# Turning the sampling matrix of a deformable convolution by DMA instead of by TensorE

## The chip, the cores and the metric

The kernel runs on one core of one Trainium2 chip. The metric is the device time of one execution in microseconds (us). TensorE (PE) multiplies matrices into PSUM, VectorE (DVE), ScalarE (ACT) and GpSimd (POOL) work elementwise, SyncE (SP) issues DMAs. Each engine works through its own instructions in order; semaphores tie them together.

## What is computed

32 images of 192 channels by 32 x 32 pixels go through channel attention and then a modulated deformable 3 x 3 convolution, each behind a group norm and with a residual; batch norm (over all 32 images) and GELU end it.

```python
x = x + attention(_gn(x))                 # q k^T over channels: 192 x 192 per image
x = x + deform(_gn(x))

def deform(x):                            # K = 9 taps
    offset = clip(_conv(x, off_w, off_b), -8, 8)
    mask = 2 * sigmoid(_conv(x, mask_w, mask_b))
    p = sum over 4 corners of  x[at the corner] * (bilinear weight * valid * mask)
    y = einsum('bckhw,ock->bohw', p, w) + b
    return gelu(batch_norm(y, over all images and pixels))
```

## The kernel before

Bilinear sampling is done as a matrix product. An image has 8 tiles of 128 pixels and 8 chunks of 128 source pixels. **Z** is a chunk of the normalized image times the projection weights, for a row of taps (`ky`) and its three `kx`: 128 source pixels by 576. **S** holds the sampling weights of a tile's 128 output pixels over 8 source rows by 32 columns, that is 256 source pixels in two halves of 128 (`c`), for three `kx`. S times Z, summed over taps and chunks, is the output (`acc`). Both are split in a high and a low float16 part, and three of the four products are formed.

Work of an image goes in 48 **units** `u` = (tile, `ky`, `c`). In each unit:

- PE `turn_s` (L666) turns three 128 x 128 float32 blocks of S of unit u+2 into PSUM bank `sps[u % 2]`, since POOL makes S with output pixels on the partitions (L1343, 128 x 768 for two units, tile `sT`) and the product wants source pixels there;
- ACT `split_s` (L905) casts them to `sh`, DVE `split_s` (L1161) subtracts to get `sl`;
- PE `convolve` (L683 to L685) does nine matmuls of 192 columns with `sh`, `sl`, `zh`, `zl`;
- PE `z_group` (L652 to L656) does five matmuls of 288 columns, a half of a Z piece, ten units ahead, into `zps[g % 2]`; ACT `split_z` (L871) casts it to `zh`, DVE `split_z` (L1155) makes `zl`. PE waits for `z_lo` of the group before last.

Behind the unit's own work stands `part0(u)`, a unit of the **preparation** of the next image: group norm, attention (gram matrix at u = 16 and 17, softmax at 18 to 20, its products at 21 and 22, applied at 23 to 26), second group norm (28), the images shifted by a pixel (`move`, DVE, u = 33, 35 and 36, L1024 to L1028, the last one raises `x2_moved`), the offset convolution on PE (u = 38 and 39, four tiles each, L594) and from u = 40 the hat functions `ay` and `bx` from which POOL makes S. An operation of u on one engine mostly waits for one of u or u-1 on another. `part1` writes out units and preparation for each engine; a loop runs over the images, two in a body. Image 0 is prepared alone, and image 31 runs without preparation. Then batch norm and GELU read y back from HBM and write the output.

SP stores and loads images (`attended`, `convolved`), nothing else.

```python
for u in range(UNITS):            # PE, part1
    turn_s(u + 2, b)
    convolve(u, b, par)
    z_group(u + AHEAD, b, par)    # AHEAD = 10 units
    if more:
        part0(u, b + 1, 1 - par)
```

Of the kernel before, what the change touches and what calls it, by code (L numbers as in the profile page):

```python
# [31 lines left out]
ALU = mybir.AluOpType  # L32
# [3 lines left out]
P = 128  # L36
# [15 lines left out]
UNITS = 6 * TILES  # L52
HEAD_SCALE = float((C // 4) ** (-0.5))
# [29 lines left out]
def build(nc, x, w_qkT, w_v, w_outT, b_out, w_off, b_off, w_proj, proj_b, gamma, beta,  # L83
# [6 lines left out]
    with ExitStack() as ctx:  # L90
# [76 lines left out]
        ST_RING = 3  # L167
        sT = sb("sT", [P, ST_RING, 3, R * W])
        S_RING = 3
        sh = sb("sh", [P, S_RING, 3, P], F16)  # L170
        sl = sb("sl", [P, S_RING, 3, P], F16)
# [13 lines left out]
        zps = bank("zps", (P, 2, 512))  # L185
        sps = [bank(f"sps{i}") for i in range(2)]
# [56 lines left out]
        s_ps = sem("s_ps")  # L243
        s_hi = sem("s_hi")
        s_lo = sem("s_lo")
        sz_done = sem("sz_done")
# [89 lines left out]
        def images(program, eng):  # L336
# [8 lines left out]
            part1(0, 0, True)  # L345
            with nc.Fori(1, NB - 2, 2, engines=bass.OrderedEngineSet([eng.engine]), hint_back_edge=True) as b:
                part1(b, 1, True)
                part1(b + 1, 0, True)
            part1(NB - 1, (NB - 1) % 2, False)
# [8 lines left out]
        AHEAD = 10  # L358
        FAR_Z = 2 * AHEAD
        FAR_SLOT = S_RING - 1  # L360
# [8 lines left out]
        def z_piece(z, g, par):  # L369

            half = g % 2 * (KO // 2)
            return z[:, tile_at(g // 6, par), g % 6 // 2, half:half + KO // 2]
# [52 lines left out]
        def _(sp):  # L425
            def load_x(b):
                for dst, src in ((xin[:, 0], x[b, 0:P]), (xin[0:CB, 1], x[b, P:C]), (xin[CB:P, 1], x[b, P:C])):
                    sp.dma_start(dst, src).then_inc(x_loaded, 16)
# [9 lines left out]
            def attended(b, more=True):  # L438
                sp.wait_ge(x1_sb, 4 * b + 4)
                sp.dma_start(x1_dram[b, 0:P], x1[:, 0]).then_inc(x1_stored, 16)  # L440
                sp.dma_start(x1_dram[b, P:C], x1[0:CB, 1]).then_inc(x1_stored, 16)
                if more:
                    load_x(b + 1)

            def convolved(b):
                sp.wait_ge(y_final, b + 1)
                sp.dma_start(y_dram[b, 0:P], ych[:, 0]).then_inc(y_stored, 16)
                sp.dma_start(y_dram[b, P:C], ych[0:CB, 1]).then_inc(y_stored, 16)

            attended(0)  # L450
            with sp.Fori(1, NB - 2, 2) as b:
                attended(b)
                convolved(b - 1)
# [956 lines left out]
```

## Time and profile before

| | us |
|---|---|
| median of 3 runs | 4003.83 (3988.3 to 4007.59) |
| the profiled execution, time | 3993.97 |
| its span, first to last instruction | 3992.2 |
| PE busy | 3544.1 (89%) |
| DVE busy | 2646.4 (66%) |
| ACT busy | 2111.3 (53%) |
| POOL busy | 1412.8 (35%) |

Busy time of PE is the union of instructions that overlap in its pipeline: a matmul of 192 columns is shown as 246 ns long, but the next starts some 80 ns later. For what a stretch of matmuls costs, starts have to be compared. Idle time before an instruction is put down to what released it.

### The profile page before, as it was taken

How to read it: one execution, taken by the hardware profiler on the slowest of the kernel's cores; microseconds unless marked ns; L12 is line 12 of the kernel's file. 1: busy time of each engine (PE TensorE's matmuls, PEld its weight loads, DVE VectorE, ACT ScalarE, POOL GpSimd, SP SyncE). 2: the span in 40 equal slices, each digit the busy share in tenths (PEclk: the TensorE clock that was granted, in tenths of full speed). 3: DMA queues.
4: the chain of work that ended last, by engine and by line, in shares of the span. 5: the costliest groups of instructions: out<-in, count | busy, mean ns of one | idle time of the engine just before them, and what ended most of it. 6: DMA issues, size and time to landing. Idle time of an engine off the chain costs nothing.

```text
span 3992.2 us, 110012 instructions
## 1 busy us (share of the span) xinstructions
PE 3544.1 (89%) x38338; PEld 3034.8 (76%) x38338; DVE 2646.4 (66%) x5834; ACT 2111.3 (53%) x4790; POOL 1412.8 (35%) x1165
## 2 busy tenths in 40 slices
PE   3999999999999999999999999999999999999700
PEld 2788887888888888888888888888888888888700
DVE  3577766676677667677766676677667667766522
ACT  1555555565555555555555565555555555555432
POOL 1333333343433333333333343333333333333311
PEclk8999999999999999999999999999999999999955
DMA  2000000000000010000000000000000001000299
GB/s 63 20 10 28 28 27 22 28 28 19 20 28 28 20 28 28 28 10 28 28 20 28 28 28 15 23 28 28 20 28 28 28 10 28 28 20 18 76 377 322
DMA packets 50722, 170.05 MB, mean 43 GB/s; under 512 B 9664, under 2 KB 10880, under 8 KB 50176
## 3 DMA queue, kind: packets, MB, share of 16 engines
q1 hardware_dynamic: 39584, 136.75, 11.2%
q0 software_dynamic: 7168, 25.17, 1.6%
q8 instruction: 337, 5.52, 0.6%
q14 instruction: 209, 1.71, 0.1%
q10 hardware_dynamic: 3424, 0.90, 0.1%
HBM read 87.29 MB, written 75.50 MB: 41 GB/s over the span
## 4 chain that ended last, share of the span: by engine, by line
PE 66%; DVE 12%; issue 9%; DMA 4%; POOL 3%; ACT 3%; DVEq 1%; SPq 1%; ACTq 0%; POOLq 0%
PE sps L666 10%; PE acc L683 6%; PE acc L685 6%; PE acc L684 6%; PE l L594 4%; PE zps L652 3%; PE zps L656 3%; PE zps L653 3%; PE zps L655 3%; PE zps L654 3%; DVE zl L1155 3%; DMA xn<-x_scratch 2%; POOL sT L1343 2%; DVE sl L1161 2%; PE l L526 2%
## 5 line engine op out<-in xcount | busy, mean ns | idle before, releaser
L1343 POOL TENSOR_TENSOR sT<-ay,bx 128x768 f32<-128x768 f32 x768 | 1149.5, 1507 | 1363.4 <-PE sps L666 1292.5
L1161 DVE TENSOR_TENSOR sl<-sps,sh 128x384 f16<-128x384 f32 x1536 | 846.0, 551 | 563.8 <-ACT sh L905 557.7
L683 PE MATMUL acc<-zh,sh 128*128 128x192 f16 x4608 | 1133.7, 246 | 0.9 <-issue 0.6
L685 PE MATMUL acc<-zh,sl 128*128 128x192 f16 x4608 | 1133.6, 246 | 0.0
L684 PE MATMUL acc<-zl,sh 128*128 128x192 f16 x4608 | 1133.6, 246 | 0.0
L905 ACT CAST sh<-sps 128x384 f16<-128x384 f32 x1536 | 741.7, 483 | 695.3 <-PE sps L666 689.6
L871 ACT CAST zh<-zps 128x288 f16<-128x288 f32 x1536 | 620.4, 404 | 638.8 <-PE zps L656 611.7
L1155 DVE TENSOR_TENSOR zl<-zps,zh 128x288 f16<-128x288 f32 x1536 | 693.2, 451 | 334.3 <-ACT zh L871 325.4
L666 PE MATMUL sps<-eye,sT 128*128 128x128 f32 x4608 | 785.8, 279 | 127.2 <-DVE sl L1161 99.4
L666 PEld LDWEIGHTS sps<-eye,sT 128*128 128x128 f32 x4608 | 530.9, 140 | 283.5 <-DVE sl L1161 167.9
L684 PEld LDWEIGHTS acc<-zl,sh 128*128 128x128 f16 x4608 | 450.9, 98 | 17.7 <-issue 0.8
L683 PEld LDWEIGHTS acc<-zh,sh 128*128 128x128 f16 x4608 | 450.8, 98 | 2.4 <-DVE sl L1161 0.5
L685 PEld LDWEIGHTS acc<-zh,sl 128*128 128x128 f16 x4608 | 450.9, 98 | 0.0
L652 PE MATMUL zps<-wpr_h,x_hi_a 128*128 128x288 f16 x1344 | 384.6, 286 | 1.0 <-DVE zl L1155 0.6
L653 PE MATMUL zps<-wpr_l,x_hi_a 128*128 128x288 f16 x1344 | 384.4, 286 | 0.0
L654 PE MATMUL zps<-wpr_h,x_lo_a 128*128 128x288 f16 x1344 | 384.4, 286 | 0.0
L655 PE MATMUL zps<-wpr_h,x_hilo_b 128*128 128x288 f16 x1344 | 384.4, 286 | 0.0
L656 PE MATMUL zps<-wpr_l,x_hilo_b 128*128 128x288 f16 x1344 | 384.4, 286 | 0.0
L1327 POOL TENSOR_TENSOR bx<-off,cx_sb 128x576 f32<-128x576 f32 x128 | 155.5, 1215 | 459.0 <-DVE off L1122 459.0
L1309 POOL TENSOR_TENSOR rstd<-gvar,mhalf 128x2 f32<-128x2 f32 x64 | 44.9, 702 | 553.9 <-DVE gvar L1012 553.9
L594 PE MATMUL l<-wof,x2s_hi_a 128*128 128x54 f16 x1536 | 182.8, 186 | 9.8 <-DVE x2w_hilo_b L1028 9.8
L594 PE MATMUL l<-wof,x2s_lo_a 128*128 128x54 f16 x1536 | 182.6, 186 | 0.0
(200 smaller groups left out, 6482.7 us busy)
## 6 DMA issues: line engine op xcount, KB each, us to landing
xin<-in_x SPq DMA_DIRECT2D x32, 512.0 KB, 5.4
xin<-in_x SPq DMA_DIRECT2D x64, 256.0 KB, 6.0
x_scratch<-x SPq DMA_DIRECT2D x32, 512.0 KB, 2.7
y_scratch<-ych SPq DMA_DIRECT2D x32, 512.0 KB, 2.7
zh<-y_scratch SPq DMA_DIRECT2D x20, 512.0 KB, 11.1
zl<-x_scratch SPq DMA_DIRECT2D x20, 512.0 KB, 12.5
out<-zh POOLq DMA_DIRECT2D x20, 512.0 KB, 8.6
x_scratch<-x SPq DMA_DIRECT2D x32, 256.0 KB, 3.4
```

Of the source, the lines that this page charges most:

```text
L594: mm = pe.matmul(o, src[:, row * W:(row + ROWS_T) * W], wof[:, m, k].rearrange("p i j -> p (i j)"), start=(k == 0 and n == 0), stop=(k == ...
L652: pe.matmul(o, at(0), wpr_h[:, 0, ky, n], start=True, stop=False)
L653: pe.matmul(o, at(0), wpr_l[:, 0, ky, n], start=False, stop=False)
L666: mm = pe.transpose(sps[u % 2][:, kx * P:(kx + 1) * P], sT[:, g, kx, c * P:(c + 1) * P], eye32[:, :])
L683: pe.matmul(acc[:, 0:C], s_h, zh[:, j, ky, z], start=start and kx == 0, stop=False)
L684: pe.matmul(acc[:, 0:C], s_h, zl[:, j, ky, z], start=False, stop=False)
L685: mm = pe.matmul(acc[:, 0:C], s_l, zh[:, j, ky, z], start=False, stop=stop and kx == 2)
L871: act.copy(z_piece(zh, g, par), zps[:, g % 2, 0:KO // 2]).then_inc(z_hi, 1)
L905: act.copy(sh[:, u % S_RING].rearrange("p k n -> p (k n)"), sps[u % 2][:, 0:3 * P]).then_inc(s_hi, 1)
L1155: dve.tensor_tensor(z_piece(zl, g, par), zps[:, g % 2, 0:KO // 2], z_piece(zh, g, par), ALU.subtract)\
L1161: dve.tensor_tensor(one(sl), sps[u % 2][:, 0:3 * P], one(sh), ALU.subtract).then_inc(s_lo, 1)
L1343: pool.tensor_tensor(sT[:, p % ST_RING].rearrange("p k (r x) -> p k r x", r=R), a, x_, ALU.mult)\
```

## The change

Turning S leaves PE. POOL writes S as float32 into `s32` (128 x 768, one **step** p = two units), ACT casts it and DVE subtracts while output pixels are still on the partitions (`spm`, 128 x 2 x 768 float16, ring of 2), and SP issues one DMA transpose per step that turns all twelve 128 x 128 blocks, high and low, SBUF to SBUF, into `sT` (ring of 4 slots). There are 24 steps per image, 768 in all. PE waits for the transpose's own semaphore. The two PSUM banks of `sps` go to `zps`, so Z is evicted 576 wide, 24 times per image on each engine. The work is written in steps; Z runs 5 steps ahead, splitting and turning 3 steps ahead, POOL 4. Preparation is shifted by 6 units (`SHIFT`): behind step p stand `part0(2p + 6)` and `part0(2p + 7)`, and units 0 to 5 of the image after the next behind steps 21 to 23. The offset convolution stands at u = 37, 38, 39 with 2, 3 and 3 tiles. SP's stores and loads now stand at step 5 (y) and at u = 36 (x), in one queue with the transposes.

```diff
+STEPS = 3 * TILES
+SHIFT = 6
-        AHEAD = 10
+        AHEAD = 5
+        S_AHEAD = 3
+            def turn_s(p, b):                                    # SP
+                sp.wait_ge(s_lo, STEPS * b + p + 1)
+                if p >= T_RING or not first(b):
+                    sp.wait_ge(sz_done, STEPS * b + p - T_RING + 1)
+                sp.dma_start_transpose(sT[:, p % T_RING], spm[:, p % S_RING].rearrange("p i n -> p (i n)"))\
+                  .then_inc(turned(b, p)[0], 16)
...
-                if 38 <= u < 40:
-                    for t in range(TILES // 2):
-                        offset_conv(TILES // 2 * (u - 38) + t, b, par)
+                if 37 <= u < 40:
+                    for t in ((0, 1), (2, 3, 4), (5, 6, 7))[u - 37]:
+                        offset_conv(t, b, par)
...
-            def turn_s(u, b):                                    # PE
-                for kx in range(3):
-                    mm = pe.transpose(sps[u % 2][:, kx * P:(kx + 1) * P], sT[:, g, kx, c * P:(c + 1) * P], eye32[:, :])
+            def convolve(p, b, par):
+                pe.wait_ge(*turned(b, p))
+                for c in range(2):
+                    mm = s_product(lambda lo, kx: sT[:, p % T_RING, 6 * lo + 2 * kx + c], ...)
...
+                for p in range(STEPS):                           # PE, part1
+                    convolve(p, b, par)
+                    z_group(p + AHEAD, b, par)
+                    for u in (2 * p, 2 * p + 1):
+                        prepare(part0, u, b, par, more)
...
+            def split_s(p, b):                                   # ACT
+                act.wait_ge(st_made, STEPS * b + p + 1)
+                if p >= S_RING or not first(b):
+                    act.wait_ge(*turned(b, p - S_RING))
+                act.copy(spm[:, p % S_RING, 0], s32[:, p % S_RING]).then_inc(s_hi, 1)
...
+            def split_s(p, b):                                   # DVE
+                dve.wait_ge(s_hi, STEPS * b + p + 1)
+                dve.tensor_tensor(spm[:, p % S_RING, 1], s32[:, p % S_RING], spm[:, p % S_RING, 0], ALU.subtract)\
+                   .then_inc(s_lo, 1)
...
+            def make_s(p, b, par):                               # POOL
+                if p >= S_RING or not first(b):
+                    pool.wait_ge(s_lo, STEPS * b + p - S_RING + 1)
```

Two places in the order of instructions. First VectorE around the last `move`, whose last copy (`x2w_hilo_b`) lets TensorE begin the offset convolution. Before, from unit 34 to unit 36 of the preparation:

```order
L1161 TENSOR_TENSOR sl<-sps,sh 128x384 [waits s_hi]
L1155 TENSOR_TENSOR zl<-zps,zh 128x288 [waits z_hi]
L1024 COPY x2s_lo_a<-x_lo_a 128x32x31 [waits xn_lo]
L1025 COPY x2s_lo_a<-x_lo_a 128x32x31
L1027 COPY x2w_lo_a<-x_lo_a 128x96
L1028 COPY x2w_lo_a<-x_lo_a 128x96
L1161 TENSOR_TENSOR sl<-sps,sh 128x384 [waits s_hi]
L1155 TENSOR_TENSOR zl<-zps,zh 128x288 [waits z_hi]
L1024 COPY x2s_hilo_b<-x_hilo_b 128x32x31
L1025 COPY x2s_hilo_b<-x_hilo_b 128x32x31
L1027 COPY x2w_hilo_b<-x_hilo_b 128x96
L1028 COPY x2w_hilo_b<-x_hilo_b 128x96
```

The same place in the changed kernel (step 15; L1193 is the low part of S, L1188 that of Z, L1255 the scaling of y):

```order
L1060 COPY x2w_lo_a<-x_lo_a 128x96
L1061 COPY x2w_lo_a<-x_lo_a 128x96
L1192 ISA
L1193 TENSOR_TENSOR spm<-s,spm 128x768 [waits s_hi]
L1187 ISA
L1188 TENSOR_TENSOR zl<-zps,zh 128x576 [waits z_hi]
L1250 ISA
L1255 TENSOR_SCALAR ych<-yt,unscale,pb 128x256 [waits yt_ps]
L1255 TENSOR_SCALAR ych<-yt,unscale,pb 128x256
L1057 COPY x2s_hilo_b<-x_hilo_b 128x32x31
L1058 COPY x2s_hilo_b<-x_hilo_b 128x32x31
L1060 COPY x2w_hilo_b<-x_hilo_b 128x96
```

The wider splits and a scaling of y now stand between the second and the third `move`.

Second TensorE ahead of the product with the softmax (u = 21), which waits for `prob_sb` of VectorE's u = 20. Before, the rows from the unit's Z group on:

```order
L652 MATMUL zps<-wpr_h,x_hi_a 128x288 [waits z_lo]
L653 MATMUL zps<-wpr_l,x_hi_a 128x288
L654 MATMUL zps<-wpr_h,x_lo_a 128x288
L655 MATMUL zps<-wpr_h,x_hilo_b 128x288
L656 MATMUL zps<-wpr_l,x_hilo_b 128x288
L619 REGISTER_ALU
L525 MATMUL l_1<-wo,gram 128x192 [waits prob_sb]
```

Now, from the end of step 7's Z group on:

```order
L704 MATMUL zps<-wpr_l,x2w_hilo_b 128x288
L730 ISA
L732 REGISTER_ALU [waits y_pm]
L734 REGISTER_ALU [waits flag_sb]
L737 MATMUL yt<-eye,ypm 128x128 [waits y_ch]
L738 MATMUL yt<-eye,ypm 128x128
L737 MATMUL yt<-eye,ypm 128x128
L738 MATMUL yt<-eye,ypm 128x128
L666 REGISTER_ALU
L572 MATMUL l_1<-wo,gram 128x192 [waits prob_sb]
```

Before, a whole unit of PE work lay between PE's place for u = 20 and that for u = 21; now both stand behind the same Z group, with only the turning of y ahead of them.

## Rows read from the trace of the kernel before

**Rows 1.** The page, its parts 1 and 2: busy time, and granted clock in 40 slices.

```profile
PE 3544.1 (89%) x38338; PEld 3034.8 (76%) x38338; DVE 2646.4 (66%) x5834; ACT 2111.3 (53%) x4790; POOL 1412.8 (35%) x1165
...
PEclk8999999999999999999999999999999999999955
```

**Rows 2.** Timeline of SP (start us, us, ...): a store of x1, 23 images apart.

```profile
878.85 0.34 SPq L440 DMA_DIRECT2D x_scratch<-x  x1
...
3530.61 0.35 SPq L440 DMA_DIRECT2D x_scratch<-x  x1
```

**Rows 3.** Groups by line and shape: xcount | busy us, mean ns | idle before <-releasers.

```profile
L1343 POOL TENSOR_TENSOR sT<-ay,bx 128x768 f32<-128x768 f32 x768 | 1149.5, 1507 | 1363.4 <-PE sps L666 1292.5 <-DVE ay L1137 37.1 <-ACT bx L864 33.7
...
L1161 DVE TENSOR_TENSOR sl<-sps,sh 128x384 f16<-128x384 f32 x1536 | 846.0, 551 | 563.8 <-ACT sh L905 557.7 <-issue 3.1
L666 PE MATMUL sps<-eye,sT 128*128 128x128 f32 x4608 | 785.8, 279 | 127.2 <-DVE sl L1161 99.4 <-POOL sT L1343 17.3 <-issue 2.7
L905 ACT CAST sh<-sps 128x384 f16<-128x384 f32 x1536 | 741.7, 483 | 695.3 <-PE sps L666 689.6
L1155 DVE TENSOR_TENSOR zl<-zps,zh 128x288 f16<-128x288 f32 x1536 | 693.2, 451 | 334.3 <-ACT zh L871 325.4
L871 ACT CAST zh<-zps 128x288 f16<-128x288 f32 x1536 | 620.4, 404 | 638.8 <-PE zps L656 611.7
```

**Rows 4.** Timeline of one unit on PE: turn, product, Z, next turn.

```profile
1001.72 0.49 PE L666 MATMUL sps<-eye,sT 128*128 128x128 f32 x3
...
1002.05 0.25 PE L683 MATMUL acc<-zh,sh 128*128 128x192 f16 x1
...
1002.79 0.29 PE L652 MATMUL zps<-wpr_h,x_hi_a 128*128 128x288 f16 x1
...
1003.40 0.49 PE L666 MATMUL sps<-eye,sT 128*128 128x128 f32 x3
```

**Rows 5.** Busy time by engine in two images: start:end, length, PE, PEld, DVE, ACT, POOL, clock.

```profile
994.50:1225.70 231.20, 221.30 (x2404) 189.72 (x2402) 161.53 (x362) 128.01 (x296) 85.36 (x68) 1.00 0.09 25
```

**Rows 6.** Operations with all inputs in SBUF, by line: ns min/median/max; ACT's as in rows 3.

```profile
L1018 DVE TENSOR_TENSOR xl_a<-xn,xh_a x32: 1224/1710/1716, 46.7 to 3596.3; 128x1024 f16<-128x1024 f32 x32
...
L1018 DVE TENSOR_TENSOR x_hilo_b<-xn,x_hilo_b x32: 1222/1222/1224, 94.2 to 3663.0; 64x1024 f16<-64x1024 f32 x32
...
L804 ACT ACTIVATE xn<-x,nbias,rstd 128x1024 f32<-128x1024 f32 x64 | 80.5, 1258 | 13.8 <-POOL nbias L1313 13.8
```

**Rows 7.** Timeline: one small DVE copy beside a POOL product, and one without.

```profile
1009.37 1.69 POOL L1343 TENSOR_TENSOR sT<-ay,bx 128x768 f32<-128x768 f32 x1 [2.23 <-PE sps L666]
...
1009.66 1.45 DVE L1027 COPY x2w_hi_a<-x_hi_a 128x96 f16<-128x96 f16 x1
...
1017.13 0.41 DVE L1024 COPY x2s_hilo_b<-x_hilo_b 128x992 f16<-128x992 f16 x1
...
1017.82 0.17 DVE L1027 COPY x2w_hilo_b<-x_hilo_b 128x96 f16<-128x96 f16 x1
```

**Rows 8.** DMA issues: xcount, KB each, median us from issue to landing.

```profile
xin<-in_x SPq DMA_DIRECT2D x32, 512.0 KB, 5.4
...
x_scratch<-x SPq DMA_DIRECT2D x32, 512.0 KB, 2.7
```

**Rows 9.** The attention chain: a group by shape, then three places of the timeline.

```profile
L525 PE MATMUL l<-wo,gram 128*128 128x192 f32 x64 | 19.2, 382 | 21.5 <-DVE gram L1075 21.5
...
1077.69 0.36 DVE L1056 COPY gram<-l 128x192 f32<-128x192 f32 x1 [1.27 <-PE l L555]
...
1089.99 1.05 DVE L1075 TENSOR_SCALAR gram<-gram,rinv 128x192 f32<-128x192 f32 x2
...
1097.58 0.56 DVE L1080 TENSOR_TENSOR mt_l<-l,mt_h 128x384 f16<-128x384 f32 x1 [1.68 <-ACT mt_h L840]
```

**Rows 10.** Timeline: u = 32 on DVE, a scaling of y, the first offset matmul.

```profile
1004.70 0.99 DVE L1223 TENSOR_SCALAR ych<-yt,unscale,pb 128x256 f32<-128x256 f32 x2
...
1006.51 1.71 DVE L1018 TENSOR_TENSOR x_lo_a<-xn,x_hi_a 128x1024 f16<-128x1024 f32 x1
...
1019.28 0.19 PE L594 MATMUL l<-wof,x2s_hi_a 128*128 128x54 f16 x1
```

More of the change, by code:

```diff
@@ L184, in build @@
         yt = bank("yt")
-        zps = bank("zps", (P, 2, 512))
-        sps = [bank(f"sps{i}") for i in range(2)]
+        zps = bank("zps", (P, 4, 512))
         l0 = [bank(f"l0_{i}") for i in range(2)]
@@ L242, in build @@
         st_made = sem("st_made")
-        s_ps = sem("s_ps")
         s_hi = sem("s_hi")
         s_lo = sem("s_lo")
+        lo_seen = sem("lo_seen")
+        slot_free = sem("slot_free")
+        s_turned = [sem(f"s_turned{i}") for i in range(T_RING)]
         sz_done = sem("sz_done")
@@ L344, in images, with prepare @@
                     weights_ready()
[L345 to L349, printed above, removed]
+            for u in range(SHIFT):
+                part0(u, 1, 1)
+            part1(0, 0, 2)
+            with nc.Fori(1, NB - 4, 2, engines=bass.OrderedEngineSet([eng.engine]), hint_back_edge=True) as b:
+                part1(b, 1, 2)
+                part1(b + 1, 0, 2)
+            for b in range(NB - 3, NB):
+                part1(b, b % 2, min(2, NB - 1 - b))
+        def prepare(part0, u, b, par, more):
+            if u + SHIFT < SLOTS:
+                if more:
+                    part0(u + SHIFT, b + 1, 1 - par)
+            elif more == 2:
+                part0(u + SHIFT - SLOTS, b + 2, par)
         far_bodies = []
@@ L678, in s_product @@
-            def s_product(slot, j, ky, start, stop):
+                for h in range(2):
+                    o = z_bank(g)[:, h]
+                    n = slice(h * KO // 2, (h + 1) * KO // 2)
+                    pe.matmul(o, at(0), wpr_h[:, 0, ky, n], start=True, stop=False)
+                    pe.matmul(o, at(0), wpr_l[:, 0, ky, n], start=False, stop=False)
+                    pe.matmul(o, at(1), wpr_h[:, 0, ky, n], start=False, stop=False)
+                    pe.matmul(o, at(2), wpr_h[:, 1, ky, n], start=False, stop=False)
+                    mm = pe.matmul(o, at(2), wpr_l[:, 1, ky, n], start=False, stop=True)
@@ L700, in far_pass @@
             def far_pass(b, par, more):
-                pe.wait_ge(s_lo, UNITS * (b + 1) + 2 * more)
                 pe.wait_ge(y_ch, 4 * (b + 1))
```

300 lines of the change are left out of this document (145 added, 155 removed).

## The prediction

> **What bounds the kernel now.** The page first: PE is busy 89% of the span, DVE 66%, and the granted clock stands at its top (tenths 9, full speed; 1.00 in the two images of [rows 5]) from the second slice to the final phase [rows 1]. The stores of x1 give the length of an image: (3530.61 - 878.85) / 23 = 115.3 us [rows 2]; 31 images run at that pace, each with the preparation of the next beside it. In one pair of them PE is busy 221.3 of 231.2 us [rows 5]. So PE's order of instructions is the path, and I read off what a unit costs there: the turn takes 2.05 - 1.72 = 0.33 us, the nine products 0.74, the five Z matmuls 0.61, together 1.68 [rows 4]. 48 units are 81 us; some 30 are preparation, and 4 to 5 PE waits. Of its waits the largest are those before the turn: 127.2 us in all, 4.0 per image, mostly for DVE's low part of S [rows 3].
>
> **Part 1: the turn leaves PE.** 48 x 0.33 = 15.8 us per image. The waits before it go too, 4.0 per image, since nothing on PE waits for a PSUM bank of `sps` any more. Together 19.8 us per image, all on the path. A step (two units) of products and Z is now 2 x (0.74 + 0.61) = 2.70 us on PE.
>
> **Part 2: splitting S 768 wide from SBUF.** ACT: 1024 elements with inputs in SBUF took 1.258 us [rows 6], so 768 take about 0.95; before, two casts of 0.483 [rows 3]. DVE: 1024 elements with both inputs in SBUF took 1.222 us undisturbed [rows 6], so 768 take 0.92, before 2 x 0.551. A gain of small size on engines that aren't the bound. But the same subtraction took 1.71 where POOL was at work [rows 6], and a DVE copy of 96 elements took 1.45 us beside a POOL product and 0.17 without one [rows 7]: it ended when the product ended. The two engines shut each other out for some forms. Before, the low part of S read one input from PSUM and took 0.551 in the mean although POOL was at work 35% of the time [rows 1, 3]; now it has two SBUF inputs, so it falls under this. I charge it half a POOL product, 0.75 (between 0 and 1.5, POOL's 1.507 of [rows 3]).
>
> The Trainium skill says the same in "Advanced Engine Details and Errata", section GPSIMD Details: POOL shares an interface with DVE and conflicts with DVE instructions in a 2-port mode or with two SBUF inputs. It speaks against this part; by [rows 6, 7] the trace agrees.
>
> **Part 3: Z evicted 576 wide.** From 288 to 384 elements ACT's cast grows by 0.079 us and DVE's subtraction by 0.100 [rows 3]; by these slopes 576 take ACT 0.64 and DVE 0.75, where two of 288 took 0.81 and 0.90. DVE's whole load: 161.53 / 2 = 80.8 us per image, less 48 x (0.551 + 0.451), plus 24 x (0.92 + 0.75 + 0.75) = 91 us. It has room under 111 us, not much. The ring of Z is two groups as before, now of double size: PE may be two steps ahead of DVE.
>
> **Part 4: the DMA transpose.** No row shows one. It carries 128 x 1536 float16, 384 KB. Plain DMAs of 512 KB took 2.7 us (store) and 5.4 (load) from issue to landing [rows 8]; by bytes 2.0 is the lower bound, 5.4 the upper one of these rows, and nothing excludes more for a turned pattern. I take 4.0, nearer to the load. It counts through a loop: `spm` has two slots, so the cast for step p + 2 waits for the transpose of p. Loop: cast 0.95 + low part 0.92 + POOL 0.75 + transpose 4.0 + some 0.5 behind other work on ACT = 7.1 us for two steps, 3.6 per step. The image needs 111 / 24 = 4.6 per step, but unevenly: the twelve steps from 17 to the next image's 4 hold little preparation, some 37 us. PE can be fed three steps from the ring there, so 9 periods must fit: up to 4.1 per period, a transpose of 5.1 us. So at 4.0 it costs nothing; above 5.1 it costs 4.5 us per image for each us of latency. SP's stores and loads stand before transposes of steps 8 and 18 or 19, where PE waits or has three steps in store: nothing.
>
> The Trainium skill ("DMA: Bandwidth & Descriptors", section Latency and other measured facts) has 261 GB/s for a DMA transpose with a broken pattern. By it the 384 KB would move in 1.5 us, the loop would be shorter than mine, and the sum would not change. No run here shows it.
>
> **Part 5: the shift and the pairing of units.** This is what I charge most. Where before an operation of u on PE waited for u-1 on another engine, a unit of 1.68 us lay between. Now u = 2p and 2p + 1 stand together behind a step's products and Z, and on ACT and DVE they stand behind the split of that same Z, which ends 0.64 + 0.75 = 1.4 us after PE's Z. Per image PE will wait:
> - u = 17 for DVE's copy of the gram matrix, 0.36 and a short second one [rows 9]: 0.6.
> - u = 21: DVE's u = 20 starts 1.4 + 0.2 behind the Z of step 7, and takes 0.2 + 1.05 [rows 9]; PE has four turns of y in between, 0.4 at a third of 0.33 each [rows 4]: 2.5. Before, 21.5 us in 32 images, 0.7 each [rows 9].
> - u = 23 for `mt_lo`, right behind its source at u = 22: ACT's two casts of 384 and 128 columns (0.48 and, by the slope of part 3, 0.27) and DVE's 0.56 and a shorter one [rows 3, 9]: 1.5; before, a unit covered it.
> - u = 37 for `x2_moved`. Count from the start of step 13 on PE. ACT has 2 x 1.26 of normalizing and 1.6 of splits in each of steps 12 and 13, 4.1 against PE's 2.7; it starts the ones of step 12 when PE starts step 13 (they follow the cast of Z), so its cast of S of step 13 ends at 0.7 + 2.5 + 0.95 = 4.1, DVE's low parts of S and Z 1.7 later, at 5.8. Then DVE: residue, behind POOL, to 7.9; move 0.9 (the undisturbed one runs from 1017.13 to 1018.0, [rows 7]), 8.8; step 14's splits behind ACT's, 10.4; residue 1.22 behind POOL, 12.4; move, 13.3; step 15's splits, 15.0; scaling of y, 0.99 [rows 10], 16.0; last move 0.9, with POOL ahead of it up to 17.3. PE is there after three steps, at 8.1, so it waits 8 (without POOL ahead of the last move) to 9.2. I take 9.2. Before, DVE ran from 1006.51 to about 1018 over the same operations, and the offset matmuls began at 1019.28 [rows 10], with hardly a wait of their own, because they stood two units behind the move; the 3 us lost there are among the 4.0 of part 1.
> - u = 12 behind a residue of 1.7 [rows 6], 1.2; and two more of this kind (u = 28 behind the moments, the turn of step 22 behind POOL's wait for the offsets), together 1.7, an estimate by the size of these.
>
> Sum 16.7; less the 1.0 that these places wait today, 15.7 net. The bounds: 0 if DVE and ACT run ahead by more than I think, and 20 if each wait behind POOL is a whole product.
>
> **The sum.** 19.8 - 15.7 = 4.1 us gained per image, 31 x 4.1 = 127 us. Against it, in the prologue six units of preparation stand uncovered and the first S goes through split and transpose before PE starts, about 8 us. Image 31 runs without preparation; its 24 steps at the loop's 3.6 less three in store take what 48 units take today, 81 us: nothing. The final phase is the same. 3994.0 (span 3992.2 and 1.8 around it) - 127 + 8 = 3875 for an execution like the profiled one; the median of the runs lies 10 us above it: **3885**.
>
> **Rivals.**
> - *The waits of part 5 are half of mine* (chance 0.20). For it: DVE is idle a third of the time today [rows 1], and delays that are added one by one, as here, may in part lie beside each other. Against: every row of the chain is measured. Then 4.1 + 8.3 = 12.4 per image: 3994 - 384 + 8 + 10, about 3630.
> - *The transpose is slow and becomes the bound* (0.18), the case on the other side. Price: with 7 us from issue to landing the period is 5.1, nine periods 46 us against 37 and PE short of S by 9 per image in place of nothing: 4.1 - 9 = -4.9, +152 us: about 4160. It decides from 6.0 us of latency on, where the 4.1 are eaten up. For it: twelve blocks per DMA are small pieces, and no row bounds them from above. Against: both plain DMAs of more bytes are under 6.
> - *DVE becomes the bound through POOL* (0.08). Each S split waits out a whole product: 91 + 24 x 0.75 = 109 us of DVE per image, and with the 8 us or so that it must wait for PE's gram and softmax products 117: +1.7 x 31 + 8 + 10, about 4065.
> - *The clock falls* (0.03). PE stands still 9 us in each image; the clock is at the lower level in the last slices, where PE has little to do [rows 1]. If each such stop cost a few us at 1.2 GHz, the gain would be gone: about 4060.
> - *It does nothing that counts* (0.04): the parts cancel, 3990 to 4020.
>
> **How the numbers follow.** My sum has the rest, 0.47, with its own range of 3780 to 4000. A measurement here can tell about 0.5% from no change, so faster means below 3984. Faster: 0.43 of the sum's 0.47, and 0.20 of the first rival, 0.63. Same: 0.03, the last rival's 0.04, and 0.05 of the cases in which the others are mild: 0.12. Slower: the rest, 0.25. The range of 3610 to 4120 leaves out the far half of the slow transpose and of the first rival.
>
> **What would show it.** Right: stores of x1 about 111 us apart; no L666 on PE; PE idle some 9 us before the first offset matmul, released by DVE's last move, and 2 to 3 before the softmax product; transposes landing in about 4 us, with no wait of PE for them in steps 0 to 16; DVE's low part of S well above 0.92 us in the mean. Wrong: transposes above 6 us, PE waiting for DMA in most steps, images above 115 us; or images at 103 us with the offset matmuls hardly waiting, which would mean that DVE's backlog in steps 13 to 15 is not what I worked out.

## The result and the profile after

The changed kernel takes **4368.97 us** in the median of 4 runs (4355.33 to 4388.95), beside 4002.81 (3988.3 to 4007.59) for the kernel before: ratio 1.0925, 95% interval 1.0874 to 1.0977. It is 9% slower. I had forecast 3885 and a range up to 4120, so both the sign and the range were wrong.

The page of the changed kernel, parts 1 and 2. Against [rows 1], PE's busy share fell from 89% to 76%, and the granted clock, steady at its top before, has eights among its nines all along.

```profile
PE 3327.8 (76%) x33730; PEld 2757.8 (63%) x33730; DVE 2413.0 (55%) x4298; ACT 1894.0 (43%) x3254; POOL 1442.3 (33%) x1165
...
PEclk8898899899898999999988999999998999888855
```

SP's stores of x1 (as [rows 2]), 21 images apart: (3261.51 - 602.51) / 21 = 126.6 us per image, before 115.3.

```profile
602.51 0.66 SPq L457 DMA_DIRECT2D x_scratch<-x  x1
...
3261.51 0.58 SPq L457 DMA_DIRECT2D x_scratch<-x  x1
```

Two images of it, columns as in [rows 5]:

```profile
1995.10:2247.90 252.80, 205.60 (x2108) 170.72 (x2108) 146.10 (x266) 114.24 (x200) 87.27 (x68) 0.91 0.54 97
```

Read this against [rows 5] per image. Before: 110.7 us busy and 5.0 idle. After: 102.8 busy and 23.6 idle, 126.4 in all. Without the turn's 15.8 us, PE should be busy 94.9 at full clock; the other 7.9 us are the lower clock (0.91 in the mean, 1.00 before). (The 94.9 rest on the 15.8 us that I read off one unit in [rows 4].) So the 10.8 us that an image got longer are made of -15.8 (the turn), +18.6 (idle) and +7.9 (clock). By the stores it is 11.3 per image, 350 of the 395 us between the two spans; the first product starts 12 us later (133.2 and 121.4), and the final phase, from the start of the last product on, is 31 us longer.

Where PE waits, from the waits of the changed kernel: who waited, for whom, us in total, times, longest.

```profile
PE acc L724 <- ACT ypm L961: 335.0, 98, 6.2
PE l L641 <- DVE x2w_hilo_b L1061: 112.0, 32, 9.8
PE l L572 <- DVE gram L1108: 95.7, 32, 3.4
PE l L564 <- DVE mv L1035: 83.3, 64, 14.2
PE l L627 <- DVE mt_l L1114: 48.9, 32, 1.5
...
PE acc L724 <- DMA sT<-spm: 7.6, 3, 6.5
```

The first row is the largest by far, and my prediction has no such term: before, the product (then L683) waited 0.3 us for this copy in the whole execution. It comes three times per image, 3.4 us each in the mean. L724 is the first matmul of a product. There is one accumulator `acc` in PSUM, and a tile's sum must be copied out of it (ACT, L960 and L961, into `ypm`) before the first product of the next tile. Here is one such place, first ACT, then PE (start us, us, engine, line, operation, [idle before]):

```profile
1979.53 1.24 ACT L838 ACTIVATE xn<-x,nbias,rstd 128x1024 f32<-128x1024 f32 x1
1980.67 1.23 ACT L829 ACTIVATE x_hi_a<-x,nbias,rstd 128x1024 f16<-128x1024 f32 x1
1981.80 0.82 ACT L938 CAST spm<-s 128x768 f16<-128x768 f32 x1
...
1984.39 1.24 ACT L838 ACTIVATE xn<-x,nbias,rstd 128x1024 f32<-128x1024 f32 x1
1985.53 1.23 ACT L829 ACTIVATE x_hilo_b<-x,nbias,rstd 128x1024 f16<-128x1024 f32 x1
1986.66 0.82 ACT L938 CAST spm<-s 128x768 f16<-128x768 f32 x1
1987.38 0.31 ACT L960 COPY ypm<-acc 128x192 f32<-128x192 f32 x1
1987.59 0.21 ACT L961 COPY ypm<-acc 128x64 f32<-128x64 f32 x1
```

```profile
1987.86 0.26 PE L724 MATMUL acc<-zh,sT 128*128 128x192 f16 x1 [3.05 <-ACT ypm L961]
...
1995.70 0.23 PE L641 MATMUL l<-wof,x2s_hi_a 128*128 128x54 f16 x1 [3.29 <-DVE x2w_hilo_b L1061]
```

ACT carries out two normalizations in each of two steps, 1.24 us apiece, and works without a pause; the copy of the tile, 0.5 us, stands behind all of it, and PE stands still. Before, the same four normalizations were spread over four units, each with PE's turn in it, and the copy was in time. Two of the three waits of an image are of this kind: 62 in the whole execution, 202 of the 335 us.

The third is another: 31 waits of 4.1 to 4.3 us, 128 us together. There ACT has no burst. It stands idle itself, for DVE's part of a row's hats (`ay`, L1159), which stands in DVE's queue behind the splits and the statistics of y, and the cast and the copy queue up behind it:

```profile
2019.25 0.44 ACT L887 ACTIVATE ay<-ay 128x288 f32<-128x288 f32 x1 [3.34 <-DVE ay L1159]
...
2020.11 0.81 ACT L938 CAST spm<-s 128x768 f16<-128x768 f32 x1
2020.83 0.31 ACT L960 COPY ypm<-acc 128x192 f32<-128x192 f32 x1
...
2021.31 0.26 PE L724 MATMUL acc<-zh,sT 128*128 128x192 f16 x1 [4.11 <-ACT ypm L961]
```

The splits and the transposes, by line (columns as in [rows 3]; the last row, of the issues, as in [rows 8]):

```profile
L1374 POOL TENSOR_TENSOR s<-ay,bx 128x768 f32<-128x768 f32 x768 | 1141.6, 1488 | 1969.5 <-DVE spm L1193 1613.2
...
L1193 DVE TENSOR_TENSOR spm<-s,spm 128x768 f16<-128x768 f32 x768 | 752.1, 979 | 627.0 <-ACT spm L938 620.5
L1188 DVE TENSOR_TENSOR zl<-zps,zh 128x576 f16<-128x576 f32 x768 | 579.4, 754 | 892.9 <-ACT zh L905 889.7
L905 ACT CAST zh<-zps 128x576 f16<-128x576 f32 x768 | 489.0, 637 | 1287.4 <-PE zps L704 1286.7
...
L938 ACT CAST spm<-s 128x768 f16<-128x768 f32 x768 | 639.5, 833 | 110.5 <-DMA sT<-spm 107.8
...
sT<-spm SPq DMA_TRANSPOSE x768, 3.7
```

And the clock, in stretches of 1 us behind that last wait (PE idle to 2021.31; the third figure from the end is the granted clock):

```profile
2021.00:2022.00 1.00, 0.69 (x9) 0.70 (x10) 1.00 (x2) 1.00 (x4) 0.01 (x1) 1.00 0.00 0
2022.00:2023.00 1.00, 1.00 (x11) 0.97 (x9) 1.00 (x2) 0.52 (x1) 1.00 (x1) 0.65 0.00 0
2023.00:2024.00 1.00, 1.00 (x7) 0.72 (x6) 0.93 (x6) 0.00 (x0) 0.47 (x1) 0.50 0.70 134
...
2026.00:2027.00 1.00, 1.00 (x15) 1.00 (x13) 0.44 (x1) 1.00 (x2) 0.20 (x1) 1.00 1.00 187
```

```profile
2022.62 0.37 PE L726 MATMUL acc<-zh,sT 128*128 128x192 f16 x1
2022.78 0.37 PE L724 MATMUL acc<-zh,sT 128*128 128x192 f16 x1
```

PE has begun again, works for about 1 us at full clock, and only then runs at 0.50, the level of 1.2 GHz, for about 3 us: matmuls of 192 columns start 0.16 us apart there (the two rows on PE), at full clock some 80 ns. In 74 of the 155 stops over 2.5 us of this trace the clock has already fallen when PE begins again, as at 2149.76. So a stop can be paid twice, once as idle time and once as slow work behind it, which the waits don't show.

### The profile page after: what moved, and what is told of

Same layout as the page of the kernel before. It is cut to its first block, busy times and chain, and to the rows that moved or that the text cites. A ratio compares the mean times of both kernels' runs of the same rounds, so it can differ in the third digit from the quotient of the medians.

```text
span 4387.3 us, 93414 instructions
## 1 busy us (share of the span) xinstructions
PE 3327.8 (76%) x33730; PEld 2757.8 (63%) x33730; DVE 2413.0 (55%) x4298; ACT 1894.0 (43%) x3254; POOL 1442.3 (33%) x1165
## 2 busy tenths in 40 slices
DMA packets 1254798, 470.63 MB, mean 107 GB/s; under 512 B 1213888, under 2 KB 1215104, under 8 KB 1254400
## 4 chain that ended last, share of the span: by engine, by line
PE 44%; DVE 15%; issue 14%; ACT 13%; DVEq 5%; DMA 5%; ACTq 3%; SPq 1%; POOL 0%; POOLq 0%
PE acc L724 6%; PE acc L725 5%; PE acc L726 5%; PE l L641 5%; ACT zh L905 3%; ACT spm L938 3%; PE zps L700 2%; DVE stats L1026 2%; PE zps L701 2%; PE zps L702 2%; PE zps L704 2%; PE zps L703 2%; DMA xn<-x_scratch 2%; ACT xn L838 2%; ACTq L897 2%
## 5 line engine op out<-in xcount | busy, mean ns | idle before, releaser
L1374 POOL TENSOR_TENSOR s<-ay,bx 128x768 f32<-128x768 f32 x768 | 1141.6, 1488 | 1969.5 <-DVE spm L1193 1613.2
L724 PE MATMUL acc<-zh,sT 128*128 128x192 f16 x4608 | 1232.9, 268 | 386.9 <-ACT ypm L961 335.0
L725 PE MATMUL acc<-zl,sT 128*128 128x192 f16 x4608 | 1233.8, 268 | 0.3 <-issue 0.3
L726 PE MATMUL acc<-zh,sT 128*128 128x192 f16 x4608 | 1233.3, 268 | 0.0
L1193 DVE TENSOR_TENSOR spm<-s,spm 128x768 f16<-128x768 f32 x768 | 752.1, 979 | 627.0 <-ACT spm L938 620.5
L1188 DVE TENSOR_TENSOR zl<-zps,zh 128x576 f16<-128x576 f32 x768 | 579.4, 754 | 892.9 <-ACT zh L905 889.7
L905 ACT CAST zh<-zps 128x576 f16<-128x576 f32 x768 | 489.0, 637 | 1287.4 <-PE zps L704 1286.7
L724 PEld LDWEIGHTS acc<-zh,sT 128*128 128x128 f16 x4608 | 489.6, 106 | 485.4 <-ACT ypm L961 319.6
L938 ACT CAST spm<-s 128x768 f16<-128x768 f32 x768 | 639.5, 833 | 110.5 <-DMA sT<-spm 107.8
L725 PEld LDWEIGHTS acc<-zl,sT 128*128 128x128 f16 x4608 | 490.9, 107 | 26.9 <-issue 0.5
L726 PEld LDWEIGHTS acc<-zh,sT 128*128 128x128 f16 x4608 | 494.6, 107 | 7.9
L641 PE MATMUL l<-wof,x2s_hi_a 128*128 128x54 f16 x1536 | 207.0, 195 | 112.0 <-DVE x2w_hilo_b L1061 112.0
L641 PE MATMUL l<-wof,x2s_hilo_b 128*128 128x54 f16 x1536 | 206.7, 195 | 0.8 <-issue 0.8
L960 ACT COPY ypm<-acc 128x192 f32<-128x192 f32 x256 | 81.4, 318 | 236.8 <-PE acc L726 236.1
## 6 DMA issues: line engine op xcount, KB each, us to landing
zl<-x_scratch SPq DMA_DIRECT2D x20, 512.0 KB, 11.3
```

Of the source, the lines that this page charges most:

```text
L641: mm = pe.matmul(o, src[:, row * W:(row + ROWS_T) * W], wof[:, m, k].rearrange("p i j -> p (i j)"), start=(k == 0 and n == 0), stop=(k == ...
L724: pe.matmul(acc[:, 0:C], s_h, zh[:, j, ky, z], start=start and kx == 0, stop=False)
L725: pe.matmul(acc[:, 0:C], s_h, zl[:, j, ky, z], start=False, stop=False)
L726: mm = pe.matmul(acc[:, 0:C], s_l, zh[:, j, ky, z], start=False, stop=stop and kx == 2)
L905: act.copy(z_piece(zh, g, par), z_bank(g)).then_inc(z_hi, 1)
L938: act.copy(spm[:, p % S_RING, 0], s32[:, p % S_RING]).then_inc(s_hi, 1)
```

## The experiments

My theory from these rows: the tile starts and the clock are what I missed; the transpose itself is innocent. The rivals: the transposes disturb the other engines or bound a loop; DVE, slowed by POOL, is behind it all; the waits for the preparation would keep PE as long if the tile starts went.

**Was the turn worth its length on PE?** The kernel before, with one turn of S per unit in place of three. Two thirds of S stay unturned, so its output is wrong. The edit:

```diff
-                for kx in range(3):
-                    mm = pe.transpose(sps[u % 2][:, kx * P:(kx + 1) * P], sT[:, g, kx, c * P:(c + 1) * P], eye32[:, :])
+                mm = pe.transpose(sps[u % 2][:, 0:P], sT[:, g, 0, c * P:(c + 1) * P], eye32[:, :])
```

> The kernel before with one 128 x 128 turn of S per unit on TensorE instead of three, which leaves out two thirds of the turning; order, splits and everything else stay. It asks what the removal alone is worth in the old order. My sum put a turn of three at 0.33 us on the path: two thirds in 48 units are 10.6 us per image, 31 images 330 us, so about 3675 if TensorE's work is the path. Theory 'TensorE's work hides the bursts of the others' (with less of it, the waits for ScalarE and VectorE come out): only half of that, 3800 to 3900. If the clock falls with TensorE's share of work, it is seen below 0.96 here as well.

Measured: 3807.4 us, ratio 0.9503 (0.9475 to 0.953). Two thirds of 15.8 us in 31 images would be 327 us; some 200 arrived. PE's busy time fell by 280 us (3544.1 to 3263.8) and its idle time grew by 92 (448.1 to 539.8). The idle time before the turn grew from the 127.2 of [rows 3]:

```profile
L665 PE MATMUL sps<-eye,sT 128*128 128x128 f32 x1536 | 453.6, 295 | 180.8 <-DVE sl L1162 155.3 <-POOL sT L1344 14.0 <-issue 6.5
```

So two things are missing from the 327: two turns cost PE's busy time less than two thirds of 0.33 us, and PE's work was also cover: with less of it per unit the other engines come late. That was the second theory of the expectation, and its range. With everything left in its place, though, the clock stays at 1.00 and most of the gain arrives.

**Are the transposes harmful in themselves?** The kernel before with 24 transposes per image of the changed kernel's shape, whose results nobody uses (it is also built with `dynamic_dma_scratch_size=4096`, as the changed kernel is):

```diff
+                    sp.dma_start_transpose(spare[:, p % 2], flat2(wpr_h).rearrange("p i n -> p (i n)")[:, 0:12 * P])\
+                      .then_inc(spared[p % 2], 16)
```

> The kernel before, with the DMA transposes added aside: in each image SyncE also issues 24 transposes of 128 x 1536 float16 from a constant tile into a spare one that nothing reads, one after each pair of low parts of S, two in flight at most. Nothing else is changed. Theory 'transposes disturb' (their traffic slows the engines, or itself lowers the granted clock): slower than before by 2% or more, clock below 0.95. Theory 'stops lower the clock, transposes are harmless': within 1% of before, clock 0.96 to 0.97; the transposes land in about 3.7 us as in the changed kernel.

Measured: 4015.58 us, ratio 1.0039 (1.0019 to 1.0059). They landed in 3.9 us in the median, 3.7 in the changed kernel. PE was busy 3545.9 us, before 3544.1, and its last product starts 3 us later (3774.1 and 3771.1). Transposes beside it cost PE next to nothing; most of the difference lies in the final phase, on which more at the end. And the loop through the transpose, with three slots of `spm` in place of two:

```diff
+        M_RING = 3
-        spm = sb("spm", [P, S_RING, 2, 3 * R * W], F16)
+        spm = sb("spm", [P, M_RING, 2, 3 * R * W], F16)
```

> The changed kernel with three slots of spm (the split S before it is turned) in place of two, so a cast of S waits for the transpose of three steps before. Theory 'the loop through the transpose is the bound': the period falls from (2 + 3.7 + queueing)/2 to a third, 3% or more faster, 4240 or less. Theory 'order of the work': the 107.8 us that ScalarE waits for the transpose go, TensorE's time barely moves: 4330 to 4380.

Measured: 4353.63 us, 1.0866 of before, where the changed kernel has 1.0925; the intervals overlap, and PE's wait for `ypm` is 329.9 us (335.0). ACT's wait for transposes fell from 107.8 us to 1.5, and PE's time barely moved: the loop doesn't bound the kernel.

**Is DVE, slowed by POOL, behind it?** The changed kernel with DVE's low part of S cut to 96 of 768 columns:

```diff
-                dve.tensor_tensor(spm[:, p % S_RING, 1], s32[:, p % S_RING], spm[:, p % S_RING, 0], ALU.subtract)\
+                dve.tensor_tensor(spm[:, p % S_RING, 1, 0:96], s32[:, p % S_RING, 0:96], spm[:, p % S_RING, 0, 0:96], ALU.subtract)\
```

> The changed kernel with VectorE's low part of S cut to 96 of its 768 columns (the rest of the low part is left out, zero): some 0.8 us less of VectorE's work per step with two inputs in SBUF, 19 us of VectorE per image. Theory 'VectorE and GpSimd in each other's way bound it': 5% faster or more, 4150. Theory 'order of the work': VectorE's work in the bursts gets shorter too, so some of the waits for it shrink, but those for ScalarE stay: 1 to 3% faster, 4240 to 4330.

Measured: 4310.91 us, 1.0784 of before. DVE's busy time fell by 559 us (2413.0 to 1854.4), the kernel by 58. DVE's load has a small part in it, as the theory 'order of the work' had it.

**The tile starts.** In the changed kernel each step's two units of preparation stand together. Pulled apart, on PE, ACT and DVE, one goes ahead of the Z group (and of its split) and one stays behind:

```diff
+                    prepare(part0, 2 * p, b, par, more)
                     if p + AHEAD < STEPS:
                         split_z(p + AHEAD, b, par)
...
-                    for u in (2 * p, 2 * p + 1):
-                        prepare(part0, u, b, par, more)
+                    prepare(part0, 2 * p + 1, b, par, more)
```

> The changed kernel with the two units of preparation of a step pulled apart: the first stands between the product (or the split of S) and Z on TensorE, ScalarE and VectorE, the second behind Z. Theory 'order of the work': what waits for the unit before gets TensorE's Z group, 1.2 us, as cover: the waits at u = 21, 23 and 37 shrink by some 1 us each per image, 3 us per image, 4270. Theory 'transposes' or 'port': no change, 4340 to 4400. A third outcome: ScalarE's and VectorE's splits of Z now stand behind a unit of preparation, so TensorE waits for Z instead, slower than 4370.

Measured: 4048.39 us, 1.0104 (1.0075 to 1.0134): 320 us of the 366 lost came back by order alone. My expectation had 4270, so it was right in its sign and far too small. The waits:

```profile
PE acc L724 <- ACT ypm L961: 178.1, 98, 4.9
PE l L564 <- DVE mv L1035: 158.7, 64, 14.2
PE l L641 <- DVE x2w_hilo_b L1061: 135.4, 32, 9.8
PE l L572 <- DVE gram L1108: 29.0, 32, 2.8
```

The tile starts, which the expectation didn't name, improve the most; the 31 of them that hang on DVE's hats fell from 128 us to 34. The softmax product (`gram`) improves too. The group statistics (`mv`) and the wait at u = 37 (112.0 before the edit), which I had expected to shrink, get worse. PE's busy time falls by 120 us, which I put down to the clock: the work is the same. The shift alone, 7 in place of 6:

```diff
-SHIFT = 6
+SHIFT = 7
```

> The changed kernel with SHIFT 7 in place of 6 and nothing else: the units that stand together become (2p+7, 2p+8), so the pairs (16,17), (20,21), (22,23), (36,37) are taken apart and (17,18), (21,22), (27,28), (3,4) are put together. Theory 'what stands together waits': TensorE's waits at u = 21, 23 and 37 (3.0, 1.5 and 3.5 us per image) shrink to below 1 us each, those before the group statistics (u = 4 and 28, L564, 2.6 us per image in the changed kernel) grow to 5 or more: net 3 us per image, about 4270. If only the number of units ahead counts, less than 1% changes.

Measured: 4194.26 us, 1.0493. The wait for `ypm` is 136.3, less than with units apart, but `mv` takes 181.7 and `xhl_b`, at u = 12, 87.1. The total came out better than the 4270 expected, again by the tile starts, which the expectation didn't name; the wait at u = 37 fell to 81.5 only. This run also says something of the clock: in its images from 700 to 3900 us no wait of PE is longer than 2.9 us, and still PE's busy time (3305.2 us) is little below the changed kernel's. Last, units apart and the tile's copy put ahead of ACT's cast of S:

```diff
+                    if p % 3 == 2:
+                        t = p // 3
+                        act.wait_ge(sz_done, STEPS * b + p + 1)
...
                     if p + S_AHEAD < STEPS:
                         split_s(p + S_AHEAD, b)
```

> The kernel with units pulled apart (4048), and ScalarE's copy of a finished tile out of the accumulator moved ahead of the cast of S in its step. TensorE there still waits 5.6 us per image at the start of a tile for this copy. Theory 'ScalarE comes late to the copy because of its bursts': the cast of S (0.83 us) no longer stands before it, 0.8 us less in some 3 waits per image, 2 us per image and a bit of clock: 3970 to 4000, faster than before. Against: the cast of S comes 0.5 us later, which costs nothing while S is three steps ahead. If the loop through the transpose is near its limit, it is 4040 to 4080.

Measured: 4154.17 us, 1.0392, so 2.6% slower than a_apart, a miss. The wait for `ypm` fell as the edit says, and others rose by more:

```profile
PE l L641 <- DVE x2w_hilo_b L1061: 172.9, 32, 9.8
PE acc L724 <- ACT ypm L953: 102.2, 92, 4.4
PE acc L724 <- DVE zl L1188: 65.3, 31, 2.5
```

By the order of instructions, ACT now waits for PE's product of this step before it casts S, which DVE and POOL wait for in turn; I take this for the cause, and no run takes it apart. The miss also says that less waiting for `ypm` isn't by itself a faster kernel: 76 us of it went here, and the kernel got slower.

**What does a stop cost by itself?** The kernel before, whose clock was at its top, with ten small DVE multiplications at u = 30 of every image:

```diff
+                if u == 30:
+                    for i in range(10):
+                        dve.drain()
+                        dve.tensor_tensor(spare[:, :], spare[:, :], spare[:, :], ALU.mult)
```

> The kernel before with a stop put in: once per image, at u = 30 of the preparation, VectorE does ten more small multiplications on a spare tile (some 6 us), so the low part of S comes late and TensorE stands still for several us. Nothing else is changed. Theory 'a stop of some us costs its length and then lowers the clock for a few us more': per image the length of TensorE's new wait plus 1.5 to 2 us, clock of the whole run below 0.95 (it is 0.966 without), and in the trace a granted clock of 0.5 behind each stop. With a new wait of 4 to 5 us per image: 4170 to 4220. Theory 'the lower clock comes with the changed kernel's other traits' (less work per unit of time on TensorE, transposes): only the wait's length, 4120 to 4160, clock 0.96.

Measured: 4241.44 us, 1.06 (1.056 to 1.0639), a little above the range of the first theory, since the stop came out at 6.5 us and not at 4 to 5. The stop in one image, the microsecond in which it ends, and the clock over 2000 us of steady work, first of this kernel, then of the kernel before:

```profile
1190.86 0.90 PE L667 MATMUL sps<-eye,sT 128*128 128x128 f32 x3 [6.53 <-DVE sl L1168]
```

```profile
1190.00:1191.00 1.00, 0.14 (x1) 0.14 (x2) 1.00 (x3) 0.00 (x0) 0.00 (x0) 0.50 0.00 0
```

```profile
1000.00:3000.00 2000.00, 1836.62 (x19504) 1575.47 (x19501) 1423.78 (x3087) 1051.40 (x2416) 696.65 (x553) 0.97 0.08 23
```

```profile
1000.00:3000.00 2000.00, 1913.28 (x20888) 1641.44 (x20887) 1397.23 (x3126) 1110.87 (x2569) 743.06 (x592) 1.00 0.08 24
```

PE's idle time grew by 162 us and its busy time, for the same matmuls, by 74 (3618.0 to 3544.1): 5.2 and 2.4 us per image. One stop per image in a kernel at full clock brings the clock down, with no other cause at hand. Here it falls in the stop, some 5 us after its start, and PE works at 0.50 for 5.6 us from 1190.86 on.

**One wait of the preparation taken back.** The changed kernel with the offset convolution in two parts again:

```diff
-                if 37 <= u < 40:
-                    for t in ((0, 1), (2, 3, 4), (5, 6, 7))[u - 37]:
-                        offset_conv(t, b, par)
+                if 38 <= u < 40:
+                    for t in range(TILES // 2):
+                        offset_conv(TILES // 2 * (u - 38) + t, b, par)
```

> The changed kernel with the offset convolution alone put back in two parts on two steps. Theory (the third part is what TensorE waits for at the offset matmuls, 3.5 us per image, and the stop costs about as much again in the clock): 4210 to 4290 us, with the wait of the offset matmuls below 40 us in all. Rival (the work before the offset maximum only crowds into one step less, and the wait moves to the hats or the tile starts): 4330 to 4390 us.

Measured: 4244.94 us, 1.0611 (1.0558 to 1.0664), with the wait for `x2_moved` at 30.9 us (before this edit 112.0) and that for `ypm` unmoved:

```profile
PE acc L724 <- ACT ypm L961: 337.3, 98, 6.1
```

PE's idle time fell by 74 us, and its busy time by another 67, although the work is the same. What b_stop showed holds in reverse: the stop gave its length back nearly twice. This was the first theory, and its range.

**A version that beats both.** Units apart, the group statistics on PE a unit later (u = 5 and 29), the offset convolution in two parts:

```diff
-                if u == 4:
+                if u == 5:
...
-                if u == 28:
+                if u == 29:
```

> The kernel with units pulled apart (4048 us), and two more waits given cover: TensorE's group statistics one unit later (u = 5 and 29 in place of 4 and 28, so that Z of the step lies before them), and the offset convolution in two parts of four tiles at u = 38 and 39 as before the change, in place of three parts from u = 37. These are the places where TensorE still stops for 5.0 and 4.2 us per image, long enough for the clock to fall behind them. Theory 'order of the work': each shrinks by 1.2 to 2.7 us, 3 to 4 us per image, and another 1 to 2 from the clock: 3860 to 3930, faster than the kernel before; clock above 0.93. If the waits only move on to the next place (the hats behind the later end of the offset convolution, the second normalization): 4000 to 4050.

Measured: **3870.71 us**, 0.9672 (0.9653 to 0.9692) of the kernel before and 11% below the changed kernel, in the range of the first theory (the clock of the four runs was 0.927 to 0.93, a little less than it had).

```profile
PE acc L724 <- ACT ypm L961: 207.3, 98, 5.2
PE l L564 <- DVE mv L1035: 82.8, 33, 14.2
PE l L641 <- DVE x2w_hilo_b L1061: 51.2, 29, 9.8
```

Three slots of `spm` on top of it:

> The same with three slots of spm in place of two, so that the cast of S waits for the transpose of three steps before. In the changed kernel this moved nothing (0.5%). With the order mended a step is shorter and ScalarE waits more for transposes (190 us with units pulled apart, against 108). Theory 'the loop through the transpose comes next': 1 to 2% faster than with two slots. Theory 'it stays hidden behind TensorE': within 0.5% of it.

Measured: 3854.63 us, 0.9633 (0.9602 to 0.9665); the intervals overlap, so this isn't told from a_v2. And a shift of 8 on top of a_v2:

> The version a_v2 (units of a step pulled apart, group statistics on their own steps, offset convolution in two parts) with a preparation shift of 8 instead of 6 and nothing else. Theory (what is left of the wait at the tile starts, 207 us for ScalarE's copy of the accumulator, is ScalarE coming late from its bursts): the shift moves the bursts against the tile starts, the wait falls by about half, some 3 us per image, and a little of the clock comes back: 3740 to 3800 us. Rival (the bursts only meet another tile start, or a wait for the group statistics or the offset matmuls grows instead): within 1% of a_v2, 3830 to 3910 us.

Measured: 3968.43 us, 0.9922 (0.9892 to 0.9952), a miss: 2.5% slower than a_v2. The first half of the theory held, the wait for `ypm` halved. But the waits inside the preparation grew by more, the one at u = 37 from 51.2 to 116.5 and the softmax product from 28.9 to 78.1. With 8 as with 6 the same units share a step; what changed is the main work that stands between them:

```profile
PE l L641 <- DVE x2w_hilo_b L1061: 116.5, 32, 9.8
PE acc L724 <- ACT ypm L961: 104.0, 85, 2.7
PE l L572 <- DVE gram L1108: 78.1, 32, 2.8
```

This was the rival's wording, though worse than its 1%. I haven't found which piece of the main work makes the difference.

Over all of them, PE's idle and busy time tell the story (us of one execution; the last column is busy time above the 3038.5 that 3544.1 - 32 x 15.8 leaves at full clock):

| | idle | busy | clock's part |
|---|---|---|---|
| changed kernel | 1059.5 | 3327.8 | 289 |
| narrow low part | 981.4 | 3326.3 | 288 |
| two parts | 985.4 | 3260.4 | 222 |
| shift 7 | 892.9 | 3305.2 | 267 |
| units apart | 839.1 | 3208.3 | 170 |
| v3 | 790.9 | 3172.8 | 134 |
| v2 | 723.5 | 3140.0 | 102 |

The last column's level rests on the 15.8 us of a turn, read off one unit; its differences don't. It doesn't follow the idle time everywhere: the narrow low part has 78 us less idle time than the changed kernel and as large a clock's part.

## Why the prediction was wrong

- **Part 1, the turn leaves PE: right about PE's work as far as the runs tell, wrong as a net gain.** 15.8 us of work went by the starts of [rows 4]; the run with one turn suggests somewhat less. The step counted it all as gained and put what it uncovered into part 5 alone.
- **Part 5, the list of waits, is the first of two steps that failed.** It went through the pairs of the preparation and left out a pair of the main work: ACT's copy of the tile and PE's next product, 10.5 us per image (335.0 / 32). All that was needed stood in my own item on u = 37. There I worked out that ACT has 4.1 us in each of steps 12 and 13 against PE's 2.7, and followed DVE behind it, but step 14 ends a tile, and its copy stands behind the same burst. The third of these waits, behind DVE's hats (128 of the 335 us), needed the same look at u = 40 and after, which the list doesn't reach. Of that item, DVE's time was right: the last `move` ends 17.3 us after the start of step 13 by my sum, 16.8 in the trace (1978.79 to 1995.55). PE's time was wrong: I had it there after 8.1, it came after 13.6, since it had stood 3.05 at the tile start and its third step took 4.6 us in place of 2.7, at a mean clock of 0.62 (1987.86 to 1992.41). So 3.3 us were left to wait where I had 9.2.
- **The other waits of part 5.** u = 21: 2.5 predicted, 3.0 measured. u = 23: 1.5 and 1.5. u = 17: 0.6 and 0.6. u = 12: 1.2, and next to nothing (4.2 us in ten images together). Two more of this kind, 1.7: the group statistics took 2.2 ((83.3 - 14.2) / 31) and the turn of the offset maximum 0.7. In sum 16.7 predicted, and 23.6 measured with the tile starts: 7 us too few.
- **The clock, a term put at nothing, is the second step that failed.** It was my rival of 0.03, sized at 4060 on its own. It is 7.9 us per image. I had seen that PE would stand still 9 us in an image, and that the clock stands lower where PE has little to do, and gave it no term because in [rows 5] it was 1.00. Nothing there stops long enough to show it: the waits for DVE's low part of S were 1.2 us at most. The Trainium skill ("TensorE: Matmul & The Clock Gate", Part 1: The HAM clock gate) has it that "the default state is throttled, and activity releases the throttle". The trace agrees: 0.50 behind the stop at 2021.31, 1.00 again after some 3 us of matmuls at 0.50. I should have weighed this rule in the prediction and didn't.
- Together: 111.2 us per image predicted, 126.6 measured; 7.9 of the difference is the clock and about 7 the waits. In 31 images that is 477 of the 514 us by which the profiled execution (4388.95) lies above my 3875; the final phase, which I had at no change, is 31. Added to 3885, the missed waits alone would give about 4100 and the clock alone about 4130. It took both to come to 4369, and they aren't independent: the stops are what brought the clock down.
- **Part 2, the charge for POOL: wrong.** The low part of S took 958 ns in the median and 979 in the mean, so some 0.05 and not 0.75 above the undisturbed 0.92. POOL's own row suggests why the rule didn't bite: POOL waits 1613.2 us for this very subtraction, since `s32` has two slots, so its product starts when the subtraction has ended and is mostly over when the next begins. The two do hinder each other when they meet: 100 of the 768 subtractions overlap a POOL instruction by more than 0.1 us; they took 1.15 us in the mean, the others 0.95. The longest one took 1697 ns. The Trainium skill's rule on the shared interface ("Advanced Engine Details and Errata", GPSIMD Details) stands by that, but a conflict needs both engines at work at the same time, which is a matter of this kernel's waits.
- **Part 3: right.** ACT 0.64 and DVE 0.75 predicted, 0.637 and 0.754 measured.
- **Part 4: right.** 4.0 us predicted, 3.7 measured; PE waits 7.6 us for transposes in the whole execution. The slow rival, a transpose above 6 us, didn't come: the sign came out as in it, the mechanism was another. That the kernel is slower was in my 0.25 for "slower", but by other mechanisms than those I had given it for.

What stays open: which length of stop brings the clock down. Most stops of this kernel at the tile starts and at u = 37, some 3 us and more, do, though not each: behind the one of 3.21 us that ends at 2051.26 it stayed at 1.00. Shorter ones do too: with a shift of 7 no wait of a steady image is above 2.9 us and the clock's part is still 267 us. With stops up to 1.4 us (the kernel with one turn) it stays at 1.00. The runs don't say where between, nor how much stops close to each other count together. Open too is what the tile starts are worth alone: no run takes away that wait and nothing else, as a second accumulator would.

## What to carry to other kernels

Work that leaves the busiest engine was also cover. Go through every pair in which that engine waits for another, those of the main loop's own buffers first (here one accumulator and its copy), and ask what stands ahead of the partner in its queue at that place. Charge a stop of TensorE of 2 or 3 us and more for more than its length (here 1.4 times in the mean, up to nearly twice), and spread bursts of the helpers over the steps before moving work: by order alone the same change went from 9% slower to 3% faster.

## What the runs showed of the hardware

- The clock can fall after a stop or in it. Behind the stop of 4.11 us PE worked at the full level for about 1 us, then about 3 us at 0.50. In the stop of 6.53 us it had fallen before PE began again, and 5.6 us of work at 0.50 followed. One such stop per image made PE's busy time 2.4 us longer.
- A DMA transpose of 128 x 1536 float16 from SBUF to SBUF landed in 3.6 us at least, 3.7 in the median and 8.9 at most; SP needed 1.43 us to issue one. 768 of them made 1,204,000 more packets (1,254,798 to 50,722) and PE's busy time in the kernel before didn't change by them. By the Trainium skill's 261 GB/s ("DMA: Bandwidth & Descriptors", Latency and other measured facts) the 384 KB would take 1.5 us, an estimate from the page's figure. The trace has more: from issue to landing they make 106 GB/s. By the packets' own times one transpose takes 2.4 us of all sixteen engines (56.7% of 4011.6 us with the unused ones, 11.2% of 3992.2 without, over 768), which is 165 GB/s, my estimate.
- The final phase, which has no transposes and the same operations, was longer in every kernel that had transposes before it: 237.5 to 252 us from the last product's start, against 219, 221 and 231 without. Here are the final phases of the kernel before, of it with the unused transposes, and of the changed kernel; DMA is fully busy in all three, and the last column is its rate in GB/s.

```profile
3780.00:3980.00 200.00, 0.00 (x0) 0.00 (x0) 54.68 (x49) 62.17 (x53) 33.35 (x61) 0.50 1.01 359
```

```profile
3795.00:4000.00 205.00, 0.00 (x0) 0.00 (x0) 52.31 (x46) 57.56 (x50) 32.94 (x60) 0.50 1.01 338
```

```profile
4150.00:4375.00 225.00, 0.00 (x0) 0.00 (x0) 52.43 (x45) 58.52 (x50) 32.85 (x60) 0.50 1.00 313
```

The same loads and stores go slower there. These are single executions, and what links them to the transposes isn't known; it wasn't tried further. Every kernel with transposes here was also built with `dynamic_dma_scratch_size=4096` and none without them was, so this argument may be the cause as well.
